# A graph network layer on one core: the column scores s_j travel through memory and are copied to PSUM by ScalarE

## The chip, the core and the metric

The kernel runs on one core of a Trainium2 chip. The core has TensorE (PE, matrix products), VectorE (DVE), ScalarE (ACT), GpSimd (POOL) and SyncE (SP), which only issues DMAs here. The metric is the device time of one launch in microseconds (us); lower is better. Three runs of the kernel before gave a median of 2245.41 us (2242.72 to 2245.51).

## The reference

128 graphs of 128 nodes with 256 features go through a layer norm with ReLU and then through three layers. Only what the change touches is named in full:

```python
h = relu(layernorm(x))
for l in range(3):
    si = h @ attn_w[l, :256]                       # one number per node
    sj = h @ attn_w[l, 256:]                       # one number per node
    scores = si[:, :, None] + sj[:, None, :] + attn_b[l]
    scores = leaky_relu(scores, 0.2), -inf where adj + eye == 0
    agg = softmax(scores) @ h
    h1 = layernorm(h + agg) * g1 + beta1
    h  = layernorm(h1 + gelu(h1 @ W1 + b1) @ W2 + b2) * g2 + beta2
out = x + h
```

With a graph's nodes i on the partitions, `si` is a column (one number per partition) and `sj` must stand along the free axis, the same row in all 128 partitions.

## The kernel before, in words

Four graphs are one group (T = 4), and one group in one layer is one item: 32 groups times 3 layers make 96 items, ordered as eight groups (RING = 8) through layer 0, the same eight through layer 1, then layer 2, then the next eight groups. Every engine runs the same list of slots. Slot s holds the feed-forward part of item s in eight chunks c = 0 to 7, and around it, at fixed chunks, the earlier stages of items s+1 to s+5 and the last stage of items s-1 and s-2. The order is written out by hand, in a `slot` function per engine; semaphores with running counts connect the engines, and there is no scheduler.

What an engine does in slot s:

- TensorE, for each chunk: `hidden` (six 128x512 matmuls into one of three PSUM banks `p_hid`, L459) and `feed` of the chunk three before (twelve 128x256 matmuls, L473). At c = 4 `spread_sj` of item s+3 (L497): four transposes of a column of `s_j`, broadcast over 128 columns, which leave `s_j` as a row in every partition of the PSUM bank `sj_bank`. At c = 6 `aggregate` of item s+2 (twelve matmuls, L511).
- ScalarE: for each chunk a Gelu in PSUM (L577) and a copy to float16 `g_hi` (L582). At c = 1 `high_X`, at 2 the norm of item s+1, at 3 `high_h` (L646) and the input norm of item s+4 where that item is of layer 0, at 5 the leaky scores of s+3 (L606, L607), at 6 their exponentials with two table loads, at 7 `high_probs`.
- VectorE: for each chunk `g_lo` (L712), which also frees the bank: TensorE's `hidden` of chunk c waits for `g_lo` of chunk c-3. Between these stand `low_probs` (L807) and the statistics of the input of item s+5 at c = 0, the residual of item s-1 (L827) at c = 1, the scores of s+3 (L776, L782) at c = 3, the attention residual of s+2 (L795) at c = 5, the eight dot products of item s+4 (L757 gives `s_i`, L760 gives `s_j`) at c = 6, and the mask of s+4 (L740, L743) at c = 7. Input statistics and mask exist for items of layer 0 only.
- GpSimd: inverse deviations (L984), norm and output of item s-2 (L1014, L1028, L1035), in the last layer also the DMA that adds x (L1042), then `X_lo`, `h_lo` (L1002) and the residual term of item s+1.
- SyncE: the DMA transposes of the probabilities (s+2) and of `h` (s+1), loads of x and of the adjacency, stores.

So a third of the slots (those that prepare items of layer 0) have more work than the others on VectorE, ScalarE and GpSimd; TensorE's work is the same in all. They are called full slots below and the others plain slots. Slots 0 to 11 and a hand-written opening before them run once with extras (weights, biases, first items); the loops repeat slots 12 to 35.

A value made in one chunk and its use in a later chunk, written as a count:

```python
if later(r, s) or c >= PF_RING:
    pe.wait_ge(g_lo_ready, total(r, s, C, c + 1 - PF_RING))
```

## Time and profile before

| what | value |
|---|---|
| median of 3 runs | 2245.41 us |
| profiled execution, its own time | 2242.66 us |
| its span in the profile | 2240.5 us |
| TensorE busy | 2195.1 us (98%) |
| GpSimd, ScalarE, VectorE busy | 1908.8, 1885.0, 1875.0 us (85, 84, 84%) |
| PE share of the chain that ended last | 90% |
| granted TensorE clock, mean | 0.997 |

The span is the time between the first and the last instruction of the profiled execution; the launch's own time is 2.2 us more. A busy time counts an engine as busy while any of its instructions runs. Matmuls overlap in the pipeline, so the pace of TensorE is read from the distance between starts, not from the duration of one.

### The profile page before, as it was taken

To read this page: it belongs to the slowest core of one execution; us is meant where nothing else is said; L and a number is where in the kernel's file an instruction comes from. 1 tells how busy PE (TensorE), PEld (TensorE's weight loads), DVE (VectorE), ACT (ScalarE), POOL (GpSimd) and SP (SyncE) were. 2 spreads that over 40 slices of the span, in tenths; PEclk is the share of its full clock that TensorE was granted. 3 is DMA by queue.
4 is the path that set the end of the run, shared out by engine and by line. 5 is a ranking of instruction groups with operands and counts; after the bars stand their busy time and mean duration, and the time that the engine had idled before them with its cause. 6 is when DMAs were issued, how large, how long until landed. Compare 5 with 4: busy or idle time off the path is not lost.

```text
span 2240.5 us, 46173 instructions
## 1 busy us (share of the span) xinstructions
PE 2195.1 (98%) x15464; PEld 1524.0 (68%) x15464; DVE 1875.0 (84%) x5886; ACT 1885.0 (84%) x3496; POOL 1908.8 (85%) x1644
## 2 busy tenths in 40 slices
PE   4999999999999999999999999999999999999998
PEld 3666766766666666676666666676666666667665
DVE  7889797888998787878999878787899978787864
ACT  6888888889998888888999888888899988888874
POOL 5888788889998888889999888888999888888886
PEclk9999999999999999999999999999999999999999
DMA  6522212145552112113655121213455211211253
GB/s 148 130 70 53 58 32 41 32 67 95 110 115 53 39 34 39 34 39 72 123 97 111 36 41 32 41 32 50 79 114 121 48 39 34 39 34 39 53 95 66
DMA packets 382266, 144.71 MB, mean 65 GB/s; under 512 B 312144, under 2 KB 380368, under 8 KB 382032
## 3 DMA queue, kind: packets, MB, share of 16 engines
q1 hardware_dynamic: 366192, 126.04, 27.0%
q0 software_dynamic: 15840, 15.73, 5.0%
q8 instruction: 125, 2.05, 0.4%
q14 instruction: 109, 0.89, 0.1%
HBM read 49.96 MB, written 16.78 MB: 30 GB/s over the span
## 4 chain that ended last, share of the span: by engine, by line
PE 90%; DVE 7%; issue 1%; ACT 1%; POOL 1%; DMA 0%; DVEq 0%; POOLq 0%; ACTq 0%
PE p_hid L459 41%; PE p_pair L473 41%; PE p_pair L511 5%; PE p_pair L497 2%; DVE bn L719 1%; DVE g_lo L712 1%; DVE dots L757 1%; DVE res L795 1%; DVE dots L760 1%; DVE p_lo L807 1%; DVE adj_in L740 0%; PE p_pair L484 0%; DVE mv L724 0%; POOL rstd L984 0%; DMA x_in<-in_x 0%
## 5 line engine op out<-in xcount | busy, mean ns | idle before, releaser
L473 PE MATMUL p_pair<-w_hi,g_hi 128*128 128x256 f16 x3072 | 838.0, 273 | 0.0
L473 PE MATMUL p_pair<-w_lo,g_hi 128*128 128x256 f16 x3072 | 838.0, 273 | 0.0
L473 PE MATMUL p_pair<-w_hi,g_lo 128*128 128x256 f16 x3072 | 837.9, 273 | 0.0
L577 ACT ACTIVATE p_hid<-p_hid,b_eff 128x512 f32<-128x512 f32 x768 | 503.1, 655 | 274.7 <-PE p_hid L459 273.5
L712 DVE TENSOR_TENSOR g_lo<-p_hid,g_hi 128x512 f16<-128x512 f32 x768 | 517.1, 682 | 45.8 <-ACT g_hi L582 38.4
L582 ACT ACTIVATE g_hi<-p_hid 128x512 f16<-128x512 f32 x768 | 458.5, 597 | 24.3
L459 PE MATMUL p_hid<-hT_hi,w_hi 128*128 128x512 f16 x1536 | 458.4, 380 | 14.4 <-DVE g_lo L712 10.6
L459 PE MATMUL p_hid<-hT_lo,w_hi 128*128 128x512 f16 x1536 | 458.2, 380 | 1.1 <-DMA hT_lo<-h_lo 1.1
L459 PE MATMUL p_hid<-hT_hi,w_lo 128*128 128x512 f16 x1536 | 458.2, 380 | 0.0
L473 PEld LDWEIGHTS p_pair<-w_lo,g_hi 128*128 128x128 f16 x3072 | 300.8, 98 | 106.7 <-issue 0.3
L473 PEld LDWEIGHTS p_pair<-w_hi,g_hi 128*128 128x128 f16 x3072 | 300.8, 98 | 106.6 <-issue 0.3
L1002 POOL TENSOR_TENSOR h_lo<-norm,h_hi 128x1024 f16<-128x1024 f32 x96 | 205.6, 2142 | 175.5 <-ACT h_hi L646 169.8
L473 PEld LDWEIGHTS p_pair<-w_hi,g_lo 128*128 128x128 f16 x3072 | 300.8, 98 | 35.0
L984 POOL TENSOR_TENSOR rstd<-var_eps,minus_half 128x4 f32<-128x4 f32 x224 | 227.9, 1017 | 83.1 <-DVE minus_mean L727 82.8
L795 DVE SCALAR_TENSOR_TENSOR res<-p_pair,row_inv,X 128x256 f32<-128x256 f32 x384 | 159.2, 477 | 151.9 <-PE p_pair L511 151.9
L459 PEld LDWEIGHTS p_hid<-hT_lo,w_hi 128*128 128x128 f16 x1536 | 150.4, 98 | 183.6 <-DMA hT_lo<-h_lo 2.0
L459 PEld LDWEIGHTS p_hid<-hT_hi,w_lo 128*128 128x128 f16 x1536 | 150.6, 98 | 182.2 <-issue 1.7
L719 DVE BATCH_NORM_STATS2 bn<-res 128x6 f32<-128x256 f32 x768 | 268.6, 411 | 3.3
L1006 POOL TENSOR_TENSOR X_lo<-X,X_hi 128x1024 f16<-128x1024 f32 x96 | 229.4, 2390 | 3.3 <-ACT X_hi L640 3.3
L996 POOL TENSOR_TENSOR h_res<-h_res,res_rows 128x1024 f32<-128x1024 f32 x96 | 225.7, 2351 | 7.5
L994 POOL TENSOR_TENSOR h_res<-norm,g_rows 128x1024 f32<-128x1024 f32 x96 | 228.0, 2375 | 4.4 <-issue 4.4
L1014 POOL TENSOR_SCALAR norm<-res,rstd,shift 128x256 f32<-128x256 f32 x380 | 205.5, 555 | 10.0
(77 smaller groups left out, 3565.3 us busy)
## 6 DMA issues: line engine op xcount, KB each, us to landing
out<-w_f SPq DMA_DIRECT2D x31, 512.0 KB, 4.8
x_in<-in_x SPq DMA_DIRECT2D x30, 512.0 KB, 4.6
w_f<-in_x POOLq DMA_DIRECT2D x30, 512.0 KB, 6.9
adj_in<-in_adj SPq DMA_DIRECT2D x32, 256.0 KB, 5.7
w_f<-in_L_gnn_W SPq DMA_DIRECT2D x6, 1024.0 KB, 7.4
hT_hi<-h_hi SPq DMA_TRANSPOSE x96, 3.1
hT_lo<-h_lo SPq DMA_TRANSPOSE x96, 3.1
pT_hi<-p_hi SPq DMA_TRANSPOSE x94, 2.4
```

The source lines that it names most:

```text
L459: mm = pe.matmul(p_hid[in_ring(s, c, PF_RING)][:], w[l][:, k, cols], h[i][:, :, k, :], start=(n == 0), stop=(n == 3 * KD - 1))
L473: mm = pe.matmul(ff_banks(s)[:, t, :], g[i][:, nodes], w[l][:, c, :], start=(c == 0 and t % 2 == 0 and n == 0), stop=(c == C - 1 and n == ...
L577: act.activation(p_hid[k][:], p_hid[k][:], ACT.Gelu, bias=b1_eff[:, l, c:c + 1], scale=1.0 / WSCALE).then_inc(gelu_ready, 1)
L582: act.activation(g_hi[i][:], p_hid[k][:], ACT.Copy).then_inc(g_hi_ready, 1)
L712: dve.tensor_tensor(g_lo[i][:], p_hid[k][:], g_hi[i][:], ALU.subtract).then_inc(g_lo_ready, 1)
L719: dve.bn_stats(bn[n][:, t, :], src[:, t, :]).then_inc(stat_steps[n], 1)
L984: pool.tensor_tensor(rstd[n][s % 2][:], var_eps[n][:], minus_half[:], ALU.pow).then_inc(rstd_ready[n], 1)
L994: pool.tensor_tensor(h_res[i][:], norm1[:], rows(g1_rows, l, T), ALU.mult).then_inc(h_res_steps, 1)
L996: pool.tensor_tensor(h_res[i][:], h_res[i][:], rows(res_rows, l, T), ALU.add).then_inc(h_res_steps, 1)
L1002: pool.tensor_tensor(h_lo[:], norm1[:], h_hi[:], ALU.subtract).then_inc(h_lo_ready, 1)
L1006: pool.tensor_tensor(X_lo[:], X[s % RING][:], X_hi[:], ALU.subtract).then_inc(X_lo_ready, 1)
L1014: pool.tensor_scalar(norm2[:, t, :], res2[:, t, :], rstd[2][s % 2][:, t:t + 1], shift[2][s % 2][:, t:t + 1], ALU.mult, ALU.add).then_inc(n ...
```

## The change

Dot products of an item are now made one slot earlier (item s+5 in slot s). SyncE writes the four `s_j` columns of the item to a scratch tensor in device memory, four bytes per node and graph, and reads them back as one row of 512 numbers broadcast to all partitions (`sj_rows`). ScalarE copies that row to the PSUM bank where the transposes used to leave it. This holds from item 5 on, the sixth; items 0 to 4 keep the transposes. Since the dot products are earlier, the input statistics, the input norm and the loads of x are one slot earlier too, and in slots 0 and 1 the additional item is fitted in. The addition of b2 to the residual row moves from VectorE to a DMA issued by GpSimd with an accumulate, so `b2_rows` disappears. The bias columns that TensorE folds in slots 2 and 7 use the other half of the PSUM pair.

```diff
+        def sj_total(r, s):
+            return total(r, s, 16, 16 - 5 * 16)
+        def bias_bank(s):
+            return pair_half(s % 2, 1)
@@ SyncE
+            def sj_to_memory(r, s):
+                sp.wait_ge(dots_ready, total(r, s, 8, 8))
+                if later(r, s, 7):
+                    sp.wait_ge(sj_in, sj_total(r, s - 2))
+                sp.dma_start(sj_memory[s % 2].rearrange("t n -> n t"), s_j[s % RING][:]).then_inc(sj_out, 16)
+            def sj_to_rows(r, s):
+                sp.wait_ge(sj_out, sj_total(r, s))
+                if later(r, s, 6):
+                    sp.wait_ge(sj_rows_ready, total(r, s - 1, 1, 1))
+                sp.dma_start(sj_rows[:].rearrange("p t n -> p (t n)"),
+                             sj_memory[s % 2].rearrange("t n -> (t n)").partition_broadcast(P)).then_inc(sj_in, 16)
             def slot(r, s):
+                if is_item(r, s + 4) and later(r, s, 2):
+                    sj_to_memory(r, s + 4)
                 if is_item(r, s + 2):
                     turn_probs_hi(r, s + 2)
                     turn_probs_lo(r, s + 2)
+                if (r, s) == (0, 1):
+                    sj_to_memory(r, s + 4)
...
                 if is_item(r, s + 1):
                     turn_h_lo(r, s + 1)
+                if is_item(r, s + 4) and later(r, s):
+                    sj_to_rows(r, s + 4)
...
                 next_adj(4)
+                next_x(6)
                 turn_h_hi(0, 0)
@@ TensorE
-                    if c == 4 and is_item(r, s + 3):
-                        spread_sj(r, s + 3)
+                    if isinstance(r, int) and r == 0 and s < 2 and c == 4:
+                        spread_sj(0, s + 3)
                     if isinstance(r, int) and (r, s, c) == (0, 0, 0):
-                        transpose_probs(1)
+                        spread_sj(0, 2)
                     if isinstance(r, int) and (r, s, c) == (0, 0, 1):
-                        spread_sj(0, 2)
                         aggregate(0, 1)
...
                 spread_sj(0, 1)
+                transpose_probs(1)
@@ ScalarE
+            def rows_to_bank(r, s):
+                act.wait_ge(sj_in, sj_total(r, s))
+                act.wait_ge(res2_ready, total(r, s - 4, 2, 2))
+                act.activation(sj_bank(r, s), sj_rows[:], ACT.Copy).then_inc(sj_rows_ready, 1)
...
+                    if c == 3 and is_item(r, s + 3) and later(r, s, 2):
+                        rows_to_bank(r, s + 3)
...
-                    if c == 3 and is_item(r, s + 4) and layer_of(s + 4) == 0:
-                        norm_input(r, s + 4)
+                    if isinstance(r, int) and (r, s, c) == (0, 0, 3):
+                        norm_input(0, 4)
+                    if c == (4 if isinstance(r, int) and (r, s) == (0, 0) else 3) and is_item(r, s + 5) and layer_of(s + 5) == 0:
+                        norm_input(r, s + 5)
@@ VectorE
-                        input_statistics(r, s + 5)
+                        input_statistics(r, s + 6)
...
-                    if c == 6 and is_item(r, s + 4):
-                        dot_products(r, s + 4, 0)
-                        dot_products(r, s + 4, 1)
+                    if isinstance(r, int) and (r, s, c) == (0, 0, 4):
+                        low_weights(0, 3)
+                        dot_products(0, 4, 0)
+                        dot_products(0, 4, 1)
+                    if isinstance(r, int) and (r, s, c) == (0, 1, 1):
+                        dot_products(0, 5, 0)
+                        dot_products(0, 5, 1)
+                    if c == 6 and is_item(r, s + 5) and not (isinstance(r, int) and (r, s) == (0, 0)):
+                        dot_products(r, s + 5, 0)
+                        dot_products(r, s + 5, 1)
+                    if isinstance(r, int) and (r, s, c) == (0, 0, 7):
+                        first_input(6)
@@ GpSimd
+            def residual_rows(layers):
+                pool.dma_start(res_rows[:, layers].rearrange("p l d -> p (l d)"),
+                               b2[layers].rearrange("l d -> (l d)").partition_broadcast(P),
+                               accum_op=ALU.add).then_inc(res_rows_ready, 16)
```

ScalarE in a plain slot before, chunks 2 to 5. `h_hi` is the float16 part of the normalized rows, `minus_max` and `leaky` belong to the scores of item s+3:

```order
L582 ACTIVATE g_hi<-p_hid 128x512
L587 ACTIVATE norm<-res,shift_1,rstd_1 128x256 x4
L577 ACTIVATE p_hid<-p_hid,b_eff 128x512
L582 ACTIVATE g_hi<-p_hid 128x512
L646 ACTIVATE h_hi<-norm 128x1024
L577 ACTIVATE p_hid<-p_hid,b_eff 128x512
L582 ACTIVATE g_hi<-p_hid 128x512
L577 ACTIVATE p_hid<-p_hid,b_eff 128x512
L582 ACTIVATE g_hi<-p_hid 128x512
L606 ACTIVATE minus_max<-row_top 128x4
L607 ACTIVATE leaky<-scores 128x512
```

The same stretch now; `p_pair<-sj_rows` is the copy of the row to PSUM:

```order
L613 ACTIVATE norm<-res,shift_0,rstd_0 128x256 x4
L603 ACTIVATE p_hid<-p_hid,b_eff 128x512
L608 ACTIVATE g_hi<-p_hid 128x512
L638 ACTIVATE p_pair<-sj_rows 128x512
L677 ACTIVATE h_hi<-norm 128x1024
L603 ACTIVATE p_hid<-p_hid,b_eff 128x512
L608 ACTIVATE g_hi<-p_hid 128x512
L603 ACTIVATE p_hid<-p_hid,b_eff 128x512
L608 ACTIVATE g_hi<-p_hid 128x512
L632 ACTIVATE minus_max<-row_top 128x4
L633 ACTIVATE leaky<-scores 128x512
```

One instruction is new, behind the copy of chunk 3 and ahead of `h_hi`; the rest keeps its place.

VectorE in slot 1 before, chunks 1 to 3. `res<-p_pair,h_res` is the feed-forward residual of item 0, `bn<-res` its statistics:

```order
L827 SCALAR_TENSOR_TENSOR res<-p_pair,h_res 128x512 x2
L712 TENSOR_TENSOR g_lo<-p_hid,g_hi 128x512
L719 BN_STATS bn<-res 128x6 x4
L712 TENSOR_TENSOR g_lo<-p_hid,g_hi 128x512
L724 BN_AGGR mv<-bn 128x2 x4
```

The same place now; the dot products of item 5 are four pairs, of which the first row and the last stand here:

```order
L858 SCALAR_TENSOR_TENSOR res<-p_pair,h_res 128x512 x2
L792 ISA dots,s_i<-X,p_rows,attn_b_col 128x256
...
L795 ISA dots,s_j<-X,p_rows 128x256
...
L747 TENSOR_TENSOR g_lo<-p_hid,g_hi 128x512
L754 BN_STATS bn<-res 128x6 x4
L747 TENSOR_TENSOR g_lo<-p_hid,g_hi 128x512
L759 BN_AGGR mv<-bn 128x2 x4
```

The dot products come in ahead of the `g_lo` of chunk 2, where nothing stood between. In slot 0, by the diff, the dot products of item 4 move from chunk 6 to chunk 4, the statistics of item 5 from chunk 4 to chunk 3, and those of item 6 come from slot 1 to chunk 7.

SyncE in a full slot before:

```order
L348 DMA_TRANSPOSE pT_hi<-p_hi 128x4x128
L354 DMA_TRANSPOSE pT_lo<-p_lo 128x4x128
L325 DMA adj_in<-in_adj 128x4x128
L330 DMA out<-w_f 128x4x256
L336 DMA_TRANSPOSE hT_hi<-h_hi 128x8x128
L322 DMA x_in<-in_x 128x4x256
L341 DMA_TRANSPOSE hT_lo<-h_lo 128x8x128
```

SyncE in a full slot now; `sj_memory<-s_j` is the write to memory, `sj_rows<-sj_memory` the read back:

```order
L372 DMA sj_memory<-s_j 128x4x1
L359 DMA_TRANSPOSE pT_hi<-p_hi 128x4x128
L365 DMA_TRANSPOSE pT_lo<-p_lo 128x4x128
L336 DMA adj_in<-in_adj 128x4x128
L341 DMA out<-w_f 128x4x256
L347 DMA_TRANSPOSE hT_hi<-h_hi 128x8x128
L333 DMA x_in<-in_x 128x4x256
L352 DMA_TRANSPOSE hT_lo<-h_lo 128x8x128
L378 DMA sj_rows<-sj_memory 128x512
```

The write stands ahead of the transposes of the probabilities, the read behind the last transpose of `h`; the seven between them are in their order from before.

## Rows read from the trace of the kernel before

**Rows 1.** The page: the span, and busy time of each engine.
```profile
span 2240.5 us, 46173 instructions
...
PE 2195.1 (98%) x15464; PEld 1524.0 (68%) x15464; DVE 1875.0 (84%) x5886; ACT 1885.0 (84%) x3496; POOL 1908.8 (85%) x1644
```
**Rows 2.** Waits of TensorE, 300 to 2200 us: total, times, longest.
```profile
PE p_hid L459 <- DVE g_lo L712: 2.2, 9, 0.3
```
**Rows 3.** Timeline of TensorE, start and duration, at the transposes of a plain slot.
```profile
998.89 0.60 PE L497 MATMUL p_pair<-ident,s_j 128*128 128x128 f32 x4
999.33 0.59 PE L459 MATMUL p_hid<-hT_hi,w_hi 128*128 128x512 f16 x2
```
**Rows 4.** Groups by line, TensorE: the transposes.
```profile
L497 PE MATMUL p_pair<-ident,s_j 128*128 128x128 f32 x384 | 59.1, 278 | 14.4 <-DVE s_j L760 13.8 <-DVE b_eff L767 0.5
```
**Rows 5.** Windows of one plain and two full slots: busy us of each engine.
```profile
988.47:1011.05 22.58, 22.58 (x162) 15.70 (x160) 18.14 (x58) 18.91 (x36) 18.74 (x17) 1.00 0.18 36
...
1124.43:1147.43 23.00, 22.76 (x162) 15.61 (x160) 22.04 (x70) 20.87 (x40) 21.90 (x20) 1.00 0.61 115
1147.43:1170.05 22.62, 22.62 (x162) 15.63 (x160) 21.66 (x70) 20.76 (x40) 21.13 (x20) 1.00 0.60 117
```
**Rows 6.** Groups by line, ScalarE: the activation nearest to the new copy.
```profile
L607 ACT ACTIVATE leaky<-scores 128x512 f32<-128x512 f32 x96 | 59.3, 618 | 0.0
```
**Rows 7.** Waits of ScalarE, then of VectorE, in three plain slots (943.29:1011.05).
```profile
ACT p_hid L577 <- PE p_hid L459: 10.1, 12, 1.7
...
DVE scores L776 <- PE p_pair L497: 3.5, 3, 1.2
```
**Rows 8.** Waits in four full slots (1101.83:1193): VectorE, GpSimd, ScalarE.
```profile
DVE res L795 <- PE p_pair L511: 2.6, 4, 0.7
...
POOL h_lo L1002 <- ACT h_hi L646: 1.4, 3, 0.6
...
ACT minus_max L606 <- DVE row_top L782: 3.0, 4, 0.8
```
**Rows 9.** Timeline of VectorE and TensorE in a plain slot.
```profile
989.41 1.28 DVE L712 TENSOR_TENSOR g_lo<-p_hid,g_hi 128x512 f16<-128x512 f32 x2
...
991.07 0.59 PE L459 MATMUL p_hid<-hT_hi,w_hi 128*128 128x512 f16 x2
```
**Rows 10.** Timeline of VectorE and TensorE in a full slot.
```profile
1154.52 0.69 DVE L712 TENSOR_TENSOR g_lo<-p_hid,g_hi 128x512 f16<-128x512 f32 x1
...
1155.27 0.61 PE L459 MATMUL p_hid<-hT_hi,w_hi 128*128 128x512 f16 x2
```
**Rows 11.** Instructions of the tile p_lo: durations min/median/max in ns.
```profile
L807 DVE TENSOR_TENSOR p_lo<-probs,p_hi x94: 677/1620/2184, 52.8 to 2167.1; 128x512 f16<-128x512 f32 x94
```
**Rows 12.** DMA issues of the page: count, KB, median us to landing.
```profile
b_col<-in_L_gnn_b SPq DMA_DIRECT2D x1, 12.0 KB, 9.2
```
**Rows 13.** Timeline of the opening, TensorE.
```profile
36.27 1.01 PE L459 MATMUL p_hid<-hT_hi,w_hi 128*128 128x512 f16 x2 [3.78 <-DMA hT_hi<-h_hi]
...
53.02 1.01 PE L459 MATMUL p_hid<-hT_hi,w_hi 128*128 128x512 f16 x2 [5.88 <-DVE g_lo L712]
...
76.80 0.60 PE L459 MATMUL p_hid<-hT_hi,w_hi 128*128 128x512 f16 x2 [1.16 <-DVE g_lo L712]
```
**Rows 14.** Timeline of the opening, ScalarE and VectorE.
```profile
38.13 0.19 ACT L618 ACTIVATION_READ_ACCUMULATOR probs<-leaky,minus_max 128x1 f32 x1
...
44.60 1.13 DVE L776 SCALAR_TENSOR_TENSOR scores<-p_pair,s_i,mask 128x128 f32<-128x128 f32 x4 [1.96 <-issue]
...
57.62 1.39 DVE L719 BATCH_NORM_STATS2 bn<-x_in 128x6 f32<-128x256 f32 x4
...
59.61 0.68 DVE L712 TENSOR_TENSOR g_lo<-p_hid,g_hi 128x512 f16<-128x512 f32 x1
...
73.09 0.47 DVE L757 CUSTOM_DVE_ANT_0 dots<-X,p_rows,attn_b_col 128x256 bf16<-128x256 f32 x1
...
76.06 1.28 DVE L712 TENSOR_TENSOR g_lo<-p_hid,g_hi 128x512 f16<-128x512 f32 x2
```

85 lines of the change are left out of this document (41 added, 44 removed).

## The prediction

> **What bounds the kernel now.** I read the page's busy times first: TensorE is busy 2195.1 of 2240.5 us, the other three about 85% [rows 1]. Then the waits of TensorE from 300 to 2200 us: only 2.2 us in all, nine times, always for a `g_lo` [rows 2]. So past the opening the time is the number of matmuls times their pace, and a matmul taken off TensorE is worth its pace, unless another engine then becomes late. The windows tell how near the others are: a plain slot lasts 22.58 us, with 18.1 us of VectorE, 18.9 of ScalarE and 18.7 of GpSimd in it; two neighbouring full slots last 23.00 and 22.62 us, with VectorE busy 22.04 and 21.66 and GpSimd 21.90 and 21.13 [rows 5]. Plain slots have room, full slots nearly none.
>
> **Term 1, the transposes.** Four transposes of a slot start at 998.89 and the next `hidden` starts at 999.33 [rows 3]: 0.44 us of TensorE's time, although the group's mean of 278 ns for one [rows 4] would suggest 4 x 0.28 = 1.1 us. The mean counts the pipeline; the starts count the pace. The group has 384 transposes for 96 items [rows 4]; items 0 to 4 keep theirs, so 91 items lose them: 91 x 0.44 = 40.0 us.
>
> **Does a plain slot give the whole 0.44 us?** TensorE's `hidden` of chunk c needs `g_lo` of chunk c-3. The tightest such pair of a plain slot is at 991.07: the `g_lo` it needs is the first of two that take 1.28 us from 989.41, done at about 990.05, so 1.0 us is left [rows 9]. That pair lies behind the exponentials, which start after `hidden` of chunk 6; the removed transposes lie at chunk 4, so both ends move up together and the 1.0 us stays. ScalarE gains one copy of 128x512. The trace has no copy from SBUF to PSUM; the nearest rows are 0.62 us for `leaky`, same size, SBUF to SBUF [rows 6], and the bounds are 0.5 and 0.7 us. I take 0.62. It goes into a slot where ScalarE waits for TensorE 10.1 us in three slots, 3.4 us each [rows 7]. Queued behind it are `h_hi` and the Gelu of chunk 4. `h_hi` 0.6 us later makes GpSimd's `h_lo` and the transposes of h later by the same; they are ready more than half a slot ahead of their use (TensorE waited for none after the opening, rows 2 have `g_lo` alone). VectorE waited for the transposes at the scores, 3.5 us in three slots [rows 7]. Now the copy ends 0.62 us behind `g_hi` of chunk 3, while VectorE spends more than that on the `g_lo` of chunk 3 (0.69 us is one such, rows 10) and on the aggregates of its statistics before it turns to the scores. So that wait goes and nothing is late in its place. Plain slots: the whole 0.44.
>
> **Full slots.** Here `g_lo` of chunk 1 runs at 1154.52 for 0.69 us and `hidden` of chunk 4 starts at 1155.27 [rows 10]: 0.06 us are left. The loop that sets the pace goes through both engines: VectorE works without a break from the attention residual at chunk 5 (where it waits for `aggregate`, 2.6 us in four slots, rows 8) to `g_lo` of chunk 1 in the next slot; TensorE then runs chunks 4, 5 and 6 up to the next `aggregate`. The transposes lie in the TensorE part, so this loop also shortens by 0.44: from 23.00 and 22.62 to 22.56 and 22.18. VectorE alone needs the slot less its wait: (23.00 + 22.62)/2 - 2.6/4 = 22.16 us on the mean, under 22.37. GpSimd's only slack is 1.4 us in four slots for `h_hi` [rows 8]: 22.81 - 0.35 = 22.46 us, 0.09 over the new pace, or 0.6 us of lag over seven full slots, which the lead of the transposes of h takes up. ScalarE's 0.62 us falls before its wait for `row_top`, 3.0 us in four slots [rows 8], 0.75 each: covered, with 0.1 to spare. If that cover is gone, what is over is exposed once a full slot: nothing to 0.5 us on about 21 slots (three groups of seven past the opening), 0 to 10 us. I take 0.
>
> **Term 2, the memory trip.** SyncE writes 512 pieces of four bytes and reads one row back to 128 partitions. No row shows such a write. A load made of 3072 four-byte pieces lands in 9.2 us [rows 12]; I take 6 us for the write, with 2 and 12 as bounds, and as much for the read. It starts when the dot products are done, around the start of a slot; the read is issued behind the last transpose of h, about half a slot on, and ScalarE wants the row at chunk 3 of the slot after: some 30 us after the dot products, against 12 us for two trips. SyncE's own order: the write stands ahead of the transposes of the probabilities, which are used 13 us or more later; the read stands ahead of the next write only. Cost 0, and no loss until a trip together with its queueing passes 30 us.
>
> The Trainium skill ("DMA: Bandwidth & Descriptors", Specifications) says that transfers under 512 B are done as read-modify-write. That speaks against four-byte writes; no row here prices it for a write, and by that rule the write would be the slower of the two trips. The sum stays, because a doubled write still ends within the slot.
>
> **Term 3, the opening.** (a) The transposes of the second item's probabilities now stand ahead of the first `hidden`, which ran at 36.27 [rows 13]; they wait for the exponentials of item 1, done at 38.3 [rows 14]. `hidden` starts about 3 us later. But `spread_sj` of item 2 comes one `hidden` sooner, and its dot products ahead of other work, so the scores of item 2, which VectorE began at 44.60 after an idle 1.96 us [rows 14], begin near 43; the first Gelu and with it TensorE's restart at 53.02, after 5.88 us of waiting [rows 13], come about 1.6 us earlier (bounds 0 and 2). (b) Between the restart and chunk 5 of slot 1 VectorE has one more set of input statistics (57.62 to 59.61, 2.0 us) and one more set of dot products (73.09 to 76.06, 3.0 us) [rows 14], 5.0 us together. Some falls into idle time of VectorE in slot 0 and into 1.16 us that TensorE waits at 76.80 anyway [rows 13]. I replayed the order by hand with these durations: `g_lo` of chunk 2 in slot 1 is late by about 2.7 us (bounds 1 and 5). (c) An extra load of x ahead of the first transpose of h: 0 to 1 us, I take 0.4. The move of the b2 row from VectorE takes about 1 us off an engine that isn't late there; the DMA for it stands in GpSimd's queue ahead of `h_lo` of item 0, which TensorE now wants later than before. Together -1.6 + 2.7 + 0.4 = +1.5 us.
>
> **Sum.** -40.0 + 1.5 = -38.5 us on the profiled execution's 2242.66 us (2240.5 of span and 2.2 around it): 2204.2. That execution lies 2.7 us under the median of the runs, 2245.41; against the median the sum is 2206.9, and I state 2207.
>
> **Rival 1: VectorE stretches in full slots.** The `p_lo` subtraction takes from 677 to 2184 ns for the same shape, median 1620 [rows 11]: it depends on what runs beside it. The phases of VectorE and GpSimd shift against each other with the change; in the four full slots read it takes about 1.15 us, so up to 1.0 us more a slot is possible, where the loop has 0.06 us of slack. On 21 slots that is 0 to 22 us; half of it gives 2218. Against it: GpSimd's order isn't touched except for one deviation a slot earlier.
>
> The Trainium skill ("SBUF — State Buffer", the section on SBUF's two separate sides) says that VectorE and GpSimd share a port pair under an exclusive lock, taken by a VectorE operation with two SBUF inputs against a GpSimd one that reads SBUF, the loser blocking for the whole instruction. The spread of `p_lo`, two SBUF inputs, agrees with it [rows 11]; it is the reason why this rival has a mechanism at all.
>
> **Rival 2: full slots fall to TensorE's own pace.** If shifted phases help, or one full slot fewer per group (statistics and masks now overlap in six slots, not seven), they come down from 22.37 to the plain 22.14: 21 x 0.23 = 4.8 us more, 2202.
>
> **Rival 3, on the other side: the row comes late.** The write waits in SyncE's queue for the dot products, the read for the write, and both share queues with loads and stores. If the trip passes the 30 us, ScalarE stands at chunk 3, and behind it the Gelus of chunks 4 on, and TensorE after its three banks. Each microsecond late costs every slot one: 91 us. From 0.5 us late on the kernel is slower than before; 1 us late gives 2207 + 91 = 2298. Against it: transposes land in about 3 us and the margin is 18 us.
>
> **Rival 4: it gives nothing.** ScalarE's copy on the path in every slot, 0.62 - 0.44 = +0.18 us x 91 = 16 us, 2262 with the transposes' gain gone. For it only that ScalarE is near full in full slots; against it 3.4 us of idle time in each plain slot [rows 7]. If only half of the slots showed it, the time would be that of before.
>
> **Chances.** Forecast 0.70; rival 1 0.14; rival 2 0.07; rival 3 0.04; rival 4 0.05. The forecast's own range is 2202 to 2213: the opening's bounds are -2 + 1 = -1 and +6, the launch spread 2.7 us. With rivals 1 and 2 the range is 2198 to 2222. 0.2% of this kernel is 4.5 us, about what a measurement can tell from none. Faster: 0.70 + 0.14 + 0.07 less a little for rival 1 with a worse opening = 0.90. Within 0.2%: 0.03. Slower: 0.07.
>
> **What would show it.** The windows of a plain slot should read 22.14 us; the group of transposes should have 20 instances; the new activation about 0.62 us, 91 times, with VectorE's wait at the scores gone and none for `sj_rows` on ScalarE. Full slots 22.2 to 22.6 us, with `p_lo` still near 1.15. The write should land in 2 to 12 us. In the opening TensorE should stop at chunk 4 or 5 of slot 1 for a `g_lo`. The forecast is wrong if plain slots stay above 22.3, if TensorE waits for `g_lo` over 10 us past 300 us, or if ScalarE waits for a DMA.

## The result, and the profile after

| | median, us | runs | ratio to before |
|---|---|---|---|
| before | 2243.19 (2242.50 to 2245.51) | 12 | |
| changed | 2250.25 (2246.02 to 2253.99) | 12 | 1.0026 [1.0018, 1.0033] |

Forecast was 2207, with 2198 to 2222 as range. The kernel became 0.26% slower: 43 us were missed. The profiled execution lasted 2247.09 us, 3.2 us under the median; its span is 2245.0. The page, as in [rows 1]:

```profile
span 2245.0 us, 45897 instructions
...
PE 2164.6 (96%) x15100; PEld 1484.3 (66%) x15100; DVE 1880.5 (84%) x5884; ACT 1931.9 (86%) x3587; POOL 1912.0 (85%) x1646
```

TensorE is busy 30.5 us less than before and the span is 4.5 us longer: TensorE stands still for 35 us more. Its waits say for whom. TensorE's waits over the whole span, then those from 300 to 2200 us, which answer to [rows 2] (engine, line waited for: us in total, times, longest):

```profile
PE p_hid L486 <- DMA hT_lo<-h_lo: 22.6, 17, 3.0
...
PE p_hid L486 <- DVE g_lo L747: 11.3, 9, 4.4
PE p_pair L571 <- ACT probs L649: 10.3, 2, 5.9
...
PE p_hid L486 <- DMA hT_hi<-h_hi: 5.2, 3, 4.7
...
PE p_pair L537 <- DMA pT_hi<-p_hi: 2.1, 3, 1.0
```
```profile
PE p_hid L486 <- DMA hT_lo<-h_lo: 20.5, 16, 3.0
...
PE p_hid L486 <- DVE g_lo L747: 1.8, 3, 0.6
```

The kernel before, over the whole span:

```profile
PE p_pair L546 <- ACT probs L618: 4.4, 1, 4.4
PE p_hid L459 <- DMA hT_hi<-h_hi: 3.8, 1, 3.8
...
PE p_hid L459 <- DMA hT_lo<-h_lo: 1.1, 1, 1.1
```

From 300 to 2200 us it waited for `g_lo` alone, 2.2 us, and the changed kernel waits for `g_lo` no longer than that. (The 3.8 us for `hT_hi` and the growth of the wait for `probs` lie in the opening, where one took the place of the other.) What is new is a wait for the DMA transposes of `h` (`hT_lo` at L352, L341 before), instructions that the change did not touch. The tile `h_lo` shows the two sides of it: how long SyncE was held at the issue (ns, min/median/max), and how long the landing took. After, and then before:

```profile
L352 SPq DMA_TRANSPOSE hT_lo<-h_lo x96: 1231/1301/11017, 36.0 to 2203.9; - x96
...
DMA to landing us min/median/max: 3.1/3.4/15.7
```
```profile
L341 SPq DMA_TRANSPOSE hT_lo<-h_lo x96: 1232/1232/2878, 36.1 to 2199.4; - x96
...
DMA to landing us min/median/max: 3.0/3.1/6.6
```

The medians hardly move, the maxima do: 15.7 us against 6.6. The worst case is the transpose that is issued in slot 1, for slot 2. SyncE there, from the timeline (start, duration):

```profile
84.98 0.39 SPq L372 DMA_DIRECT2D sj_memory<-s_j  x1
85.41 0.50 SPq L336 DMA_DIRECT2D adj_in<-in_adj  x1
86.01 1.24 SPq L347 DMA_TRANSPOSE hT_hi<-h_hi  x1
87.29 0.57 SPq L333 DMA_DIRECT2D x_in<-in_x  x1
87.91 11.02 SPq L352 DMA_TRANSPOSE hT_lo<-h_lo  x1
```

and TensorE behind it:

```profile
99.65 1.04 PE L486 MATMUL p_hid<-hT_hi,w_hi 128*128 128x512 f16 x2 [4.75 <-DMA hT_hi<-h_hi]
...
103.62 1.04 PE L486 MATMUL p_hid<-hT_lo,w_hi 128*128 128x512 f16 x2 [2.08 <-DMA hT_lo<-h_lo]
```

The issue of one transpose holds SyncE for 11 us; between it and the new write of `s_j` stand three other transfers. That TensorE's two matmuls then take 1.04 us instead of 0.6 is its clock at half speed after the idle time: the granted clock from 99 to 107 us is 0.50. The windows tell what the DMA engines do meanwhile (the last three columns are granted clock, DMA share, GB/s; the DMA share counts packets in flight and can pass 1):

```profile
85.00:90.00 5.00, 4.39 (x29) 2.80 (x30) 4.90 (x18) 2.90 (x6) 4.92 (x3) 1.00 1.00 56
90.00:95.00 5.00, 4.91 (x40) 3.58 (x37) 4.93 (x15) 4.92 (x14) 4.75 (x5) 1.00 1.76 13
```

From 90 to 95 us packets are in flight all the time and 13 GB/s are moved. The same windows in the kernel that is like this one but does not write `s_j` (e1_no_write below):

```profile
85.00:90.00 5.00, 4.48 (x30) 2.88 (x31) 4.90 (x18) 2.91 (x7) 4.92 (x3) 1.00 0.72 187
90.00:95.00 5.00, 5.00 (x41) 3.79 (x39) 4.93 (x15) 4.92 (x14) 4.71 (x5) 1.00 0.93 272
```

The same loads move 187 and 272 GB/s. This pair of rows is the miss in small: the transfers are issued, and hardly a byte gets through.

In the full slots the transposes of `h` are issued later after the write: `hT_hi` 8 to 12 us after it, `hT_lo` 12 to 16 us. What stands between is the load of the adjacency and the store, and these move slowly. From 1.7 us after the issue of that load on, two microseconds in one full slot of the changed kernel and in the same slot of e1_no_write:

```profile
596.40:598.40 2.00, 2.00 (x14) 1.21 (x13) 2.00 (x5) 1.97 (x5) 1.97 (x1) 1.00 0.81 79
```
```profile
581.70:583.70 2.00, 2.00 (x15) 1.23 (x13) 2.00 (x5) 1.97 (x5) 1.70 (x3) 1.00 0.96 314
```

79 GB/s against 314. In that slot `hT_lo` was then held 5.8 us at its issue and landed 9.0 us after it, where 3.1 is the median without the write.

What the prediction said of TensorE itself held. One plain slot and one full one, as in [rows 5], and the copy and the transposes left, as in [rows 6] and [rows 4]:

```profile
985.00:1007.15 22.15, 22.15 (x157) 15.27 (x156) 18.16 (x57) 19.44 (x36) 18.72 (x17) 1.00 0.24 48
1103.30:1127.00 23.70, 22.45 (x158) 15.19 (x157) 21.79 (x67) 21.22 (x41) 21.77 (x20) 1.00 0.73 122
```
```profile
L638 ACT ACTIVATE p_pair<-sj_rows 128x512 f32<-128x512 f32 x91 | 54.3, 597 | 8.6 <-DVE res L858 6.6 <-issue 1.8
...
L521 PE MATMUL p_pair<-ident,s_j 128*128 128x128 f32 x20 | 4.4, 363 | 13.7 <-DVE s_j L795 13.7
```

The plain slot lasts 22.15 us, TensorE busy throughout. The full slot lasts 23.70 where 22.2 to 22.6 were forecast, 1.25 us of it without TensorE. To see where the 43 us lie I took the distance between the `hidden` of chunk 7 of neighbouring slots, for three kernels (e3_no_trip below has neither write nor read):

| slots | changed against before | e3_no_trip against before | what the trip costs |
|---|---|---|---|
| the first eight | +10.7 us | -1.1 us | 11.8 |
| 32 slots in and beside the full ones | +10.0 | -13.8 | 23.8 |
| the others | -14.8 | -21.8 | 7.0 |

One slot of the opening has nearly all of the first row: 35.71 us, 25.55 without the trip. Plain slots are hit too, more rarely: one lasts 26.05 us, with 2.08 us of standstill of TensorE ahead of `aggregate`, which uses the transposes of the probabilities; the issue of `pT_lo`, right behind the write, had been held 4.0 us there.

### The profile page after: what moved, and what is told of

Same layout as the page of the kernel before. It is cut to its first block, busy times and chain, and to the rows that moved or that the text cites. A ratio compares the mean times of both kernels' runs of the same rounds, so it can differ in the third digit from the quotient of the medians.

```text
span 2245.0 us, 45897 instructions
## 1 busy us (share of the span) xinstructions
PE 2164.6 (96%) x15100; PEld 1484.3 (66%) x15100; DVE 1880.5 (84%) x5884; ACT 1931.9 (86%) x3587; POOL 1912.0 (85%) x1646
## 4 chain that ended last, share of the span: by engine, by line
PE 81%; DMA 8%; DVE 5%; ACT 2%; issue 1%; SPq 1%; another core or an unknown queue 0%; POOL 0%; DVEq 0%; ACTq 0%; POOLq 0%
PE p_hid L486 38%; PE p_pair L500 38%; DMA hT_lo<-h_lo 6%; PE p_pair L537 4%; DMA pT_hi<-p_hi 2%; DVE dots L792 1%; DVE bn L754 1%; DVE g_lo L747 1%; DVE res L830 1%; DVE dots L795 1%; SPq L333 0%; ACT norm L613 0%; ACT X L613 0%; ACT p_hid L603 0%; PE p_pair L511 0%
## 5 line engine op out<-in xcount | busy, mean ns | idle before, releaser
L486 PE MATMUL p_hid<-hT_lo,w_hi 128*128 128x512 f16 x1536 | 458.9, 380 | 22.8 <-DMA hT_lo<-h_lo 22.6
L1041 POOL TENSOR_TENSOR X_lo<-X,X_hi 128x1024 f16<-128x1024 f32 x96 | 223.4, 2327 | 9.7 <-ACT X_hi L671 9.7
```

The source lines that it names most:

```text
L486: mm = pe.matmul(p_hid[in_ring(s, c, PF_RING)][:], w[l][:, k, cols], h[i][:, :, k, :], start=(n == 0), stop=(n == 3 * KD - 1))
L1041: pool.tensor_tensor(X_lo[:], X[s % RING][:], X_hi[:], ALU.subtract).then_inc(X_lo_ready, 1)
```

## The experiments

Three theories were put up. A: the write of `s_j`, 512 pieces of four bytes, holds up the DMAs that come after it. B: the read does, 128 rows of 2 KB. C: neither; the opening and the work moved a slot ahead cost what the transposes gave back. Each kernel was measured beside the kernel before, which had a median of 2243.2 to 2243.4 us each time but the last (2245.4). The kernels without the write, without the read back, or with only part of the row written compute other scores than the reference.

### Which half of the trip

e1_no_write leaves the write out and reads 2 KB of x in place of `s_j`:

```diff
-                    sp.dma_start(sj_memory[s % 2].rearrange("t n -> n t"), s_j[s % RING][:]).then_inc(sj_out, 16)
...
-                             sj_memory[s % 2].rearrange("t n -> (t n)").partition_broadcast(P)).then_inc(sj_in, 16)
+                             x[0, 0:2].rearrange("n d -> (n d)").partition_broadcast(P)).then_inc(sj_in, 16)
```

> The changed kernel without the four-byte writes to memory; the read of one row per item stays, but it reads the first 512 numbers of x, so the column scores are not those of the reference. Theory A (the 512 four-byte writes of an item are accepted quickly but take some 8 us to settle in memory, and transposes and loads queued behind them land late in full slots and in slot 2): the full slots fall to 22.2 to 22.6 us, slot 2 waits for no transpose of h, 2206 to 2216 us. Theory B (the 256 KB read back per item crowds the queues): almost nothing changes, 2240 to 2250 us. Theory C (the shift by one slot and the new opening order are the cause): 2240 to 2250 us.

Measured: 2204.97 us, 0.9826 [0.9811, 0.984]. TensorE's wait for `hT_lo` falls to 1.2 us.

e2_no_read keeps the write and reads one row of x once only, for item 5; the scores use that row throughout. Where the write waited for a read, it now waits for the write two items before.

```diff
             def sj_to_rows(r, s):
+                if not (isinstance(r, int) and (r, s) == (0, 5)):
+                    return
```

> The changed kernel with the four-byte writes of every item, but the row is read back once only, for item 5; ScalarE copies that row for every item, so the scores of the later items are not those of the reference. Theory A: nearly nothing is won, 2238 to 2250 us, full slots still near 23.5. Theory B: 2206 to 2216 us. Theory C: 2240 to 2250 us.

Measured: 2242.62 us, 0.9994 [0.9985, 1.0003]; the wait for `hT_lo` stays at 18.4 us.

e3_no_trip has neither: e1's edit and e2's together.

> The changed kernel without writes and with a single read of x; ScalarE copies the same row for every item, so the column scores are not those of the reference. What is left is the gain of the transposes, ScalarE's copy, the shift and the new opening. Theories A and B: 2203 to 2212 us, plain slots 22.15, full slots 22.2 to 22.6. Theory C: 2240 us or more, full slots still at 23.5 or slot 2 still at 35 us.

Measured: 2204.88 us, 0.9827 [0.9811, 0.9843]. So the read alone costs nothing that could be measured (e1 and e3 differ by 0.1 us, each one's runs by 2.3 to 2.8), the write alone 37.7 us (e2 less e3), and both together 45. B falls. With the write there the read adds 7.6 us; a row that is read while the write holds memory up is one more transfer that waits, but no run tells that apart.

g1_transposes turns the other way: the whole change stays but for the trip, and the transposes are back on TensorE, in chunk 4 for item s+3.

```diff
...
-                    if isinstance(r, int) and r == 0 and s < 2 and c == 4:
-                        spread_sj(0, s + 3)
+                    if c == 4 and is_item(r, s + 3):
+                        spread_sj(r, s + 3)
...
```

> The changed kernel with the four transposes per item back on TensorE for all items and no trip through memory; the shift by one slot, the new opening and the row addition by DMA stay. All outputs are those of the reference. The kernel without trip took 2204.9 us; 91 x 0.44 = 40 us come back: 2243 to 2247 us, the same as the kernel before within 0.2%. If the shift and the new opening had a cost of their own, it would show here above 2248.

Measured: 2244.45 us, 1.0005 [0.9995, 1.0014]. The shift and the new opening cost 1.3 us, 3 at the upper end of the interval: C falls as the cause of 43 us. From g1 to e3, where the transposes go and ScalarE's copy comes, it is 39.6 us; 91 x 0.44 = 40.0 were forecast.

### What of the write it is

e4_nodes_first lays memory out by nodes, so that a node's four numbers are one piece of 16 bytes: 128 pieces, the same 2 KB. ScalarE's copy puts them in order.

```diff
-        sj_memory = [nc.dram_tensor(f"sj_memory{i}", [T, N], F32).ap() for i in range(2)]
+        sj_memory = [nc.dram_tensor(f"sj_memory{i}", [N, T], F32).ap() for i in range(2)]
...
-                    sp.dma_start(sj_memory[s % 2].rearrange("t n -> n t"), s_j[s % RING][:]).then_inc(sj_out, 16)
+                    sp.dma_start(sj_memory[s % 2], s_j[s % RING][:]).then_inc(sj_out, 16)
...
-                act.activation(sj_bank(r, s), sj_rows[:], ACT.Copy).then_inc(sj_rows_ready, 1)
+                act.activation(sj_bank(r, s), sj_rows[:].rearrange("p t n -> p (t n)").rearrange("p (n t) -> p t n", t=T), ACT.Copy).then_inc(sj_rows_ready, 1)
```

> The changed kernel with the scratch tensor laid out node by node: 128 pieces of 16 bytes instead of 512 of four bytes; ScalarE's copy does the rearrangement in its read pattern. All outputs are those of the reference. Theory A: a quarter of the pieces settles in about 2 us instead of 8, 2207 to 2222 us. Theory B and C: 2245 to 2252 us. A side risk is that the strided read makes the copy slower than the 0.60 us measured.

Measured: 2209.57 us, 0.9845 [0.983, 0.986]. The same place of slot 1 on SyncE:

```profile
84.99 0.34 SPq L372 DMA_DIRECT2D sj_memory<-s_j  x1
...
87.81 2.84 SPq L352 DMA_TRANSPOSE hT_lo<-h_lo  x1
```

2.84 us instead of 11.02. This is the whole computation, 34 us faster than the kernel before and 41 faster than the changed one.

f1_apart keeps 512 pieces of four bytes and no read, as e2, but lays each 512 bytes from the next:

```diff
-        sj_memory = [nc.dram_tensor(f"sj_memory{i}", [T, N], F32).ap() for i in range(2)]
+        sj_memory = [nc.dram_tensor(f"sj_memory{i}", [T, N, 128], F32).ap() for i in range(2)]
...
-                    sp.dma_start(sj_memory[s % 2].rearrange("t n -> n t"), s_j[s % RING][:]).then_inc(sj_out, 16)
+                    sp.dma_start(sj_memory[s % 2][:, :, 0].rearrange("t n -> n t"), s_j[s % RING][:]).then_inc(sj_out, 16)
```

> The kernel without the read back (one read of x at item 5, ScalarE copies that row for every item, so the column scores are not those of the reference), with the four-byte writes 512 bytes apart instead of next to each other; 512 of them per item as before. Its partner has the same 512 writes side by side in 2 KB and took 2242.6 us. Theory A1 (writes to the same small stretch of memory wait for each other): 2204 to 2215 us. Theory A2 (each small write costs the same wherever it goes): 2238 to 2250 us. In between would say that both count.

Measured: 2205.27 us, 0.9831 [0.9816, 0.9846]. The number of pieces and their size alone are not the price. It matters where they land. The same edit with `[T, N, 16]` is g2_64_apart, with `[T, N, 4]` g3_16_apart, with `[T, N, 2]` h3_8_apart:

> As the kernel with writes 512 bytes apart (2205.3 us; no read back, ScalarE copies one fixed row, so the column scores are not those of the reference), with 64 bytes between the four-byte writes: 512 of them in 32 KB. If writes wait for each other only where they fall into the same small piece of memory of at most 64 bytes: 2204 to 2209 us. If the piece is larger: 2212 us or more.

Measured: 2204.57 us, 0.9829 [0.9814, 0.9843].

> The same with 16 bytes between the writes, 512 of them in 8 KB. If a piece of 64 bytes is what they wait for, four writes share one instead of sixteen: 2207 to 2220 us. If side by side is all that matters: 2205.

Measured: 2203.99 us, 0.9828 [0.9812, 0.9844].

> Four-byte writes eight bytes apart, no read back (x read once). 16 bytes apart cost nothing (2204.0), side by side 2242.6. If the cost belongs to pieces whose neighbours share the same small block of memory and it halves with their number in a block, 2215 to 2230; if only strictly adjacent pieces are slow, 2204 to 2206; if a block of 16 bytes or more is what is shared, 2240.

Measured: 2205.58 us, 0.9829 [0.9813, 0.9845].

g4_half writes two of the four graphs, 256 pieces side by side in 1 KB:

```diff
-                    sp.dma_start(sj_memory[s % 2].rearrange("t n -> n t"), s_j[s % RING][:]).then_inc(sj_out, 16)
+                    sp.dma_start(sj_memory[s % 2][0:2].rearrange("t n -> n t"), s_j[s % RING][:, 0:2]).then_inc(sj_out, 16)
```

> The kernel without read back (2242.6 us) with only two of four graphs written: 256 four-byte writes side by side in 1 KB, one fixed row copied by ScalarE, so the column scores are not those of the reference. If the delay is a sum over the writes, it halves to some 4 us and most of it is hidden: 2206 to 2225 us. If it is set by how many fall into one piece, which is sixteen as before, it stays 2235 to 2245 us.

Measured: 2236.61 us, 0.997 [0.9961, 0.9979]. Half as many pieces still cost 31.7 of the 37.7 us.

i1_pairs writes pairs that touch (nodes m and m + 64), 16 bytes from pair to pair, into `[T, N // 2, 4]`; the halves of a pair come from two issues, one behind the other:

```diff
-                    sp.dma_start(sj_memory[s % 2].rearrange("t n -> n t"), s_j[s % RING][:]).then_inc(sj_out, 16)
+                    for half in range(2):
+                        sp.dma_start(sj_memory[s % 2][:, :, half].rearrange("t m -> m t"), s_j[s % RING][64 * half:64 * half + 64, :]).then_inc(sj_out, 16)
```

> Four-byte writes in pairs: the numbers of nodes m and m + 64 lie side by side, each pair 16 bytes from the next; two issues of 256 pieces, nothing read back. As dense on the whole as h3_8_apart (8 of 16 bytes written, in 4 KB), which cost nothing. If what costs is that two pieces touch, this one costs about as much as side by side, 2225 to 2243. If it is how many bytes of a stretch of memory are written, or whether the whole falls into 2 KB, it costs nothing, 2204 to 2207 (the second issue takes SyncE some 0.4 us a slot, which nothing waits for).

Measured: 2205.53 us, 0.9833 [0.9816, 0.9849]. That two pieces touch is not enough, at least when they are written one issue apart.

j1_far_graphs keeps each graph's 128 pieces side by side but puts the four graphs 8 KB apart:

```diff
-        sj_memory = [nc.dram_tensor(f"sj_memory{i}", [T, N], F32).ap() for i in range(2)]
+        sj_memory = [nc.dram_tensor(f"sj_memory{i}", [T, 2048], F32).ap() for i in range(2)]
...
-                    sp.dma_start(sj_memory[s % 2].rearrange("t n -> n t"), s_j[s % RING][:]).then_inc(sj_out, 16)
+                    sp.dma_start(sj_memory[s % 2][:, 0:N].rearrange("t n -> n t"), s_j[s % RING][:]).then_inc(sj_out, 16)
```

> As e2_no_read (512 four-byte pieces, x read once), but the 512 bytes of each graph lie 8 KB from those of the next: inside a graph the nodes stay side by side, and the whole no longer falls into 2 KB. If long unbroken runs of touching four-byte pieces are slow, 2236 to 2243 as before. If it is that all pieces fall into one or two KB of memory at one time, 2204 to 2210.

Measured: 2996.19 us (2973.11 to 3004.97), 1.336 [1.3335, 1.3386]. Neither theory had that: +754 us on e2. Its waits, TensorE for the transposes of the probabilities, which stand right behind the write on SyncE:

```profile
PE p_pair L540 <- DMA pT_hi<-p_hi: 409.0, 70, 9.2
```

and its chain, 51% of which is this transfer (before, TensorE had 90%):

```profile
DMA 52%; DVE 21%; PE 19%; issue 6%; SPq 1%; another core or an unknown queue 0%; ACT 0%; POOL 0%; DVEq 0%; POOLq 0%; ACTq 0%
DMA pT_hi<-p_hi 51%; PE p_pair L540 8%; PE p_pair L503 5%; PE p_hid L489 5%; DVE res L833 5%; DVE dots L795 4%; DVE dots L798 4%; DVE bn L757 3%; DVE g_lo L750 2%; DMA hT_lo<-h_lo 1%; SPq L373 1%; DVE mv L762 1%; DMA pT_lo<-p_lo 1%; DVE var_eps L764 0%
```

### How long a write is felt

The trace records every DMA packet. The engines' own instructions come in packets of 8 KB on a queue of their own, so they show how the other transfers fare without SyncE's queue. Mean duration in ns of those that begin in the given time after the first packet of a write, 0.9 us after its issue (2 to 22 packets each); the last column but one is how long the write itself took from its issue to its landing, as a median in us:

| kernel | where the pieces land | 0-2 us | 2-4 | 4-6 | 6-8 | 8-10 | 10-14 | write lands | time, us |
|---|---|---|---|---|---|---|---|---|---|
| f1_apart | 512 B apart | 515 | 439 | 348 | 442 | 496 | 380 | 1.8 | 2205.3 |
| g3_16_apart | 16 B | 939 | 542 | 445 | 481 | 413 | 364 | 2.7 | 2204.0 |
| i1_pairs | pairs, 16 B | 1001 | 1094 | 611 | 399 | 424 | 382 | 2.8 | 2205.5 |
| h3_8_apart | 8 B | 1569 | 1206 | 658 | 467 | 521 | 366 | 4.0 | 2205.6 |
| e2_no_read | side by side | 2056 | 2934 | 2110 | 2972 | 2007 | 397 | 10.0 | 2242.6 |
| j1_far_graphs | side by side, graphs 8 KB apart | 1529 | 1481 | 1681 | 5152 | 3298 | 2874 | 19.7 | 2996.2 |

The 512 pieces themselves are recorded as 7 to 9 ns each and over within 1.5 us. The landings are the last semaphore update of each write; in e2 and j1 the trace lacks part of these updates, so 10.0 and 19.7 us are rather too short. What the pieces leave behind is felt by packets of another queue about as long as the write is under way: for 2 us at 16 bytes, 4 us at 8 bytes and for the pairs, 10 us side by side, over 14 us in j1. Inside one stretch of memory, the denser the pieces lie, the longer it lasts; j1, as dense in each stretch and lasting twice as long, does not fit into this and is not explained. In the changed kernel itself the write landed after 10.0 us, as in e2. In g4_half, with half the pieces, it took 8.5.

Theory A holds, with one correction: not the size of the pieces makes the price but small size and dense place together. Why the median time jumps only between 8 bytes and side by side is argued, not shown: within 4 us of the write there stand, slot 1 apart, only the transposes of the probabilities, used 13 us or more later, while a hold-up of 10 us reaches the load and the store of the full slots, and with them the transposes of `h` behind these.

### Order, queue and place

i2_node_fours is h1 below, but `s_j`'s numbers lie 8 bytes apart in SBUF, so that the 16 bytes of a node are four pieces of four, issued one after another:

```diff
-        s_j = [sb(f"s_j{i}", [P, T]) for i in range(RING)]
+        s_j = [sb(f"s_j{i}", [P, T, 2])[:, :, 0] for i in range(RING)]
```

> As h1_strided_scores, the whole computation, but s_j's numbers lie 8 bytes apart in SBUF, so that a node's 16 bytes are written as four pieces of four bytes that touch and are issued one after the other. In e2_no_read the pieces that touch belong to neighbouring nodes and are issued four apart. If every row of touching four-byte pieces is slow, 2238 to 2250; if it is only the order (neighbours written by different DMA engines at one time), near h1's 2204.5, 2203 to 2208.

Measured: 2216.08 us, 0.9876 [0.9862, 0.9891], 11.6 us above h1 and between the two times that were expected. The packets of 8 KB are slow for 6 us (1658, 2025, 1895 ns, then 765), and the write lands after 7.0 us. So the order matters too: the same dense 2 KB cost a quarter of the 45 us when neighbours are written in turn (both with the read back).

f2_other_queue issues the write from ScalarE at chunk 0, not from SyncE:

```diff
...
+                    if c == (2 if isinstance(r, int) and (r, s) == (0, 1) else 0) and is_item(r, s + 4) and later(r, s):
+                        sj_to_memory(r, s + 4)
```

> The changed kernel with the four-byte write issued by ScalarE at chunk 0 instead of SyncE ahead of the transposes; same pieces, same memory, all outputs those of the reference. Theory A (the writes slow everything that shares the DMA engines and the memory, whichever queue they come from): 2243 to 2256 us, instruction fetches of 8 KB still over 1 us on the mean. Theory Q (only what stands behind them in SyncE's queue is held up): 2207 to 2225 us.

Measured: 2239.21 us, 0.9983 [0.9974, 0.9993], 4 us under theory A's range and 14 over theory Q's; TensorE still waits 20.2 us for `hT_lo`. A block in SyncE's queue is not the cause: the hold-up comes from a write in another queue as well.

f3_four_behind moves the write on SyncE from ahead of the transposes of the probabilities to behind them, which is nearer to the transposes of `h` (`hT_hi` is issued 4.8 us after the write on the median, 9.0 in the changed kernel):

```diff
-                if is_item(r, s + 4) and later(r, s, 2):
-                    sj_to_memory(r, s + 4)
                 if is_item(r, s + 2):
                     turn_probs_hi(r, s + 2)
                     turn_probs_lo(r, s + 2)
-                if (r, s) == (0, 1):
+                if is_item(r, s + 4) and later(r, s):
                     sj_to_memory(r, s + 4)
```

> The changed kernel with the four-byte write behind the two transposes of the probabilities instead of ahead of them, in every slot. Theory A: the writes settle some microseconds later in the slot, nearer to the load of the adjacency, the store and the transposes of h, so it is no better: 2248 to 2275 us. Theory Q (it matters only that transposes of the probabilities stand behind the write): 2215 to 2235 us.

Measured: 2318.95 us, 1.0339 [1.0324, 1.0354]: worse, as theory A said, but far beyond its 2275; theory Q falls. TensorE waits for both:

```profile
PE p_hid L484 <- DMA hT_hi<-h_hi: 52.6, 24, 6.1
PE p_hid L484 <- DMA hT_lo<-h_lo: 30.9, 24, 2.9
```

f4_nodes_behind has f3's edit on e4, with its 16-byte pieces:

> The version with pieces of 16 bytes (2209.6 us) with the write behind the two transposes of the probabilities. The 4.6 us that it stands over the kernel without writes should be what its 128 pieces still cost; moved behind, they meet loads instead: 2208 to 2214 us by theory A, 2205 by theory Q. All outputs are those of the reference.

Measured: 2210.1 us, 0.9853 [0.9836, 0.9869], as e4. What a dense write of small pieces costs goes by what follows it within 10 us; with pieces of 16 bytes the same move of the write cost nothing.

### The 4.6 us that e4 had left, and the fastest version

h2_strided_copy is e1_no_write with e4's edit of the copy (its last pair of lines) and nothing else of e4:

> e1_no_write (no write, the read takes a row of x instead) with the copy to PSUM reading at a distance of 16 bytes, as e4 does. If the copy is what e4 lost, the time is that of e4, 2209 to 2210, with a copy of 1097 ns. If the pieces were, it is that of e1, 2205, although the copy takes 1097 ns.

Measured: 2208.13 us, 0.9841 [0.9827, 0.9856]: 3.2 of the 4.6 us are the copy's. h1_strided_scores is e4 with the copy straight, and VectorE's scores read the bank at 16-byte distance (against e4):

```diff
-                act.activation(sj_bank(r, s), sj_rows[:].rearrange("p t n -> p (t n)").rearrange("p (n t) -> p t n", t=T), ACT.Copy).then_inc(sj_rows_ready, 1)
+                act.activation(sj_bank(r, s), sj_rows[:], ACT.Copy).then_inc(sj_rows_ready, 1)
...
+                rows = sj_bank(r, s)
+                if not (isinstance(r, int) and r == 0 and s < 5):
+                    rows = rows.rearrange("p t n -> p (t n)").rearrange("p (n t) -> p t n", t=T)
...
```

> As e4_nodes_first (16 bytes of each node written, 2209.6 us), but ScalarE copies the row to PSUM as it lies in memory and VectorE's scores read the PSUM bank with a distance of 16 bytes. If the 4.6 us that e4 lies above e1_no_write are its copy, whose read at 16-byte distance takes 1097 ns instead of 597, they go: 2205 (2203 to 2207), copy near 600 ns, VectorE's score step still near 341 ns. If a 16-byte piece itself holds others up a little, the time stays at 2209 to 2210. If VectorE pays for the distance as ScalarE did, the score step doubles to some 680 ns, 1.4 us more an item, and full slots lengthen: 2220 or more.

Measured: 2204.53 us (2203.0 to 2207.24), 0.9827 [0.9812, 0.9841]: the whole computation in the time that the kernels without any write need, and 2.5 us under the 2207 that was forecast for the change. The groups by line, the copy of e4, then copy and score step of h1:

```profile
L638 ACT ACTIVATE p_pair<-sj_rows 128x512 f32<-128x512 f32 x91 | 99.9, 1097 | 16.1 <-DVE res L858 15.8
```
```profile
L638 ACT ACTIVATE p_pair<-sj_rows 128x512 f32<-128x512 f32 x91 | 54.3, 597 | 12.6 <-DVE res L861 12.6
...
L814 DVE SCALAR_TENSOR_TENSOR scores<-p_pair,s_i,mask 128x128 f32<-128x128 f32 x384 | 107.4, 342 | 2.8 <-issue 1.4 <-PE p_pair L521 1.3
```

ScalarE pays for the distance in SBUF (1097 against 597 ns), VectorE does not for the one in PSUM (342 against 341 ns with the row in order, as in e4).

## Why the prediction was wrong, step by step

**What bounds the kernel: right.** In the changed kernel as in the one before, time is TensorE's matmuls plus its standstills; but the chain that ended last now runs through DMAs for 8% of the span, where it was 0%.

**Term 1, the transposes, -40.0 us: right.** Plain slots went from 22.59 to 22.15 us (22.14 forecast); 39.6 us between g1 and e3. In full slots the forecast was too small: without the trip thirteen of the eighteen distances that were 23.0 or 22.6 us are 22.15, instead of 22.56 and 22.18; the first of each round is 22.40 to 22.50, and two of the fifteen others stand out with 22.62 and 23.36. On the whole they fell to TensorE's own pace, as rival 2 had it. The prediction's count of 21 slots was too high: before, only three slots a round, nine in all, stood at 23.0, and the ones between them at the plain 22.6. One plain slot a round became 0.3 us longer (22.92) where it should have lost 0.44, and 23.22 in g1_transposes, so it belongs to the shift; it was not foreseen and is not explained.

**ScalarE's copy, 0.62 us, covered: right** on both counts: 597 ns, and in three plain slots ScalarE's wait for TensorE is 7.6 us where it was 10.1 [rows 7], 0.83 us a slot less; the copy of 0.60 still fits. VectorE's wait at the scores for TensorE fell from 70.6 us over the whole span to 1.3.

**Term 2, the memory trip, "Cost 0, and no loss until a trip together with its queueing passes 30 us": this step failed.** The row itself came in time: the write landed after 10.0 us (2 to 12 forecast), the read after 3.7, and over the whole trace ScalarE never waits for the read back. But the sum asked of the trip only whether it reaches its own reader, and priced nothing of what it does to the other transfers. A write of four-byte pieces side by side slows the other DMAs for 10 us after it, those of other queues too. In slot 1 the transposes of `h` are issued 1 and 3 us after the write; in full slots the load and the store fall into the 10 us and the transposes of `h` queue up behind them, with little to spare: 22.6 us of waits for `hT_lo` and 5.2 for `hT_hi`, and TensorE's clock at half speed after the long ones (0.50 from 99 to 107 us, 0.72 on the mean from 1574 to 1578). Measured price: 45 us for the trip (2250.25 less 2204.88). The nearest row, [rows 12], a load of 12 KB in 3072 four-byte pieces that needs 9.2 us, I took as the time of a trip and not as a time for which other transfers could be held up; no row of before shows what such a write does to them, so this term needed a run and not a zero.

The Trainium skill ("DMA: Bandwidth & Descriptors", Specifications) says that transfers under 512 B are done as read-modify-write, and I let it stand with "the sum stays, because a doubled write still ends within the slot". The runs show no price per piece: 512 four-byte writes 512 bytes apart land in 1.8 us and cost nothing (2205.27 us). That many read-modify-writes to the same small stretch must take turns would fit the table by distance; it is an inference, no run shows the memory at work, and j1 does not follow from it.

**Term 3, the opening, +1.5 us: near in its sum, in part by luck.** g1_transposes, with the shift and the new opening and without the trip, shows it alone. Its chunk 7 of slot 0 starts 1.4 us earlier than before, and the eight slots after it are together 1.5 us longer, where -1.2 and +2.7 were forecast: 0.2 us for the opening instead of 1.5. What g1 lost besides, 1.9 us in its profiled execution, lies in the three plain slots of 23.22 us, for which the prediction had no term. TensorE's restart in the changed kernel came at 51.30 us instead of 53.02 [rows 13], 1.7 us earlier (1.6 forecast):

```profile
51.30 1.01 PE L486 MATMUL p_hid<-hT_hi,w_hi 128*128 128x512 f16 x2 [4.37 <-DVE g_lo L747]
```

**The rivals.** Rival 1, VectorE stretching: not it. TensorE waits 1.8 us for `g_lo` past 300 us, and `p_lo` has the same spread as in [rows 11]:

```profile
L842 DVE TENSOR_TENSOR p_lo<-probs,p_hi x94: 681/1632/2019, 51.1 to 2171.6; 128x512 f16<-128x512 f32 x94
```

Rival 3 had the right part of the kernel, the trip, and the right sign, but another mechanism: the row does not come late. Rival 4 at half ("the time of before") came near the measured time, by luck: its reason, ScalarE's copy on the path, is wrong. The rivals shared one gap: each looked for the loss at the engines or at the new row itself, none at the transfers that merely run beside. So did the three signs by which the forecast was to be known as wrong (plain slots above 22.3 us, over 10 us of waits for `g_lo`, ScalarE waiting for a DMA): none of them came, save in the few plain slots named above, and the forecast was wrong all the same. Only the full slots, 23.70 us where 22.2 to 22.6 were expected, told.

## What to carry to other kernels

A new DMA is priced twice: when it lands for its reader, and what it does to the transfers issued after it (here for 10 us). When a strided write scatters four-byte elements densely, turn the layout so that each partition writes its bytes in one piece, and undo the order on the reading side, on the engine that gets it for nothing (here VectorE out of PSUM). When a wait appears on a DMA that the change did not touch, look at windows with a high DMA share and few GB/s, and at what was issued in the 10 to 15 us ahead.

## What the runs showed of the hardware beyond that

- 512 four-byte writes per slot cost, over e1's 2205 us: nothing at a distance of 8, 16, 64 or 512 bytes; 11.6 us side by side if a node's four follow each other (with the read back, over h1); 37.7 us side by side if neighbours are issued four apart; 791 us if in addition the four stretches lie 8 KB from each other. That 8 KB makes it 21 times worse is not explained; a distance of other than 8 KB was not tried. The Trainium skill ("DMA: Bandwidth & Descriptors", Latency and other measured facts) reports slower copies at row distances of large powers of two, from 512 KiB on, and takes memory channels that coincide for the reason without having verified it; 8 KB is far below that, and four-byte pieces are another case.
- Before, 242 of the 256-byte packets of the transposes took over 1 us; 1126 after, 917 in e2_no_read, 3668 in j1_far_graphs.
- ScalarE's activation of 128x512 from SBUF at a 16-byte distance took 1097 ns, contiguous 597 ns.
- An issue on SyncE can be held for 11 us by transfers in flight: the duration of the issue row itself (L352, 11.02 us) is the sign.
